# A vision transformer tower on one core: queries' and keys' product ahead of the payload's turn, and the exponential per tile

## The reference

```python
h = tokens(x)                                      # patches @ W.T + b, class token, + pos_embed
h = h + attention(layernorm(h))
h = h + experts(layernorm(h))

# attention, per head: window of 2 * 6 + 1 keys
scores = einsum('bnhd,bnwhd->bnhw', q, k_win) * D ** -0.5     # masked outside the image
out = einsum('bnhw,bnwhd->bnhd', softmax(scores), v_win).reshape(B, N, C) @ w_proj + b_proj

# experts
probs = softmax(flat @ router_w.T)
top_w, top_i = top_k(probs, 2)                     # normalised to sum 1
out = sum over e of w_e * (gelu(flat @ w1[e] + b1[e]) @ w2[e] + b2[e])
```

## Time and profile before

| | us |
|---|---|
| median of 3 runs | 1504.02 (1502.65 to 1506.02) |
| profiled execution | 1507.62 |
| its span | 1505.8 |
| busy in the span: TensorE | 1400.3 (93%) |
| VectorE | 1119.4 (74%) |
| GpSimd | 913.9 (61%) |
| ScalarE | 664.8 (44%) |

### The profile page before, as it was taken

How to read it: one execution, slowest core, us unless ns; L and a number is a source line. 1 busy time by engine, 2 the same in 40 slices (tenths; PEclk the granted TensorE clock), 3 DMA queues, 4 the chain that set the end, 5 groups by cost and what they waited for, 6 DMA issues and landing times.

```text
span 1505.8 us, 50706 instructions
## 1 busy us (share of the span) xinstructions
PE 1400.3 (93%) x17454; PEld 1165.2 (77%) x17455; DVE 1119.4 (74%) x2828; ACT 664.8 (44%) x1148; POOL 913.9 (61%) x902
## 2 busy tenths in 40 slices
PE   5899999999999999999788999999999999999995
PEld 5788788888888888888666677777777777777774
DVE  2578788898888888889677777666666666666663
ACT  2455555554555455455554434333333333333331
POOL 4235666666666667666367866666655666666565
PEclk9999999999999999999899999999999999999998
DMA  5565575767665675755355585555555555554553
GB/s 168 169 195 157 156 195 167 210 168 193 167 196 158 179 202 162 197 165 162 75 99 100 97 142 79 75 75 75 75 72 73 74 74 75 74 74 71 72 73 32
DMA packets 305660, 189.14 MB, mean 126 GB/s; under 512 B 201977, under 2 KB 291397, under 8 KB 304477
## 3 DMA queue, kind: packets, MB, share of 16 engines
q1 hardware_dynamic: 241706, 118.06, 32.2%
q0 software_dynamic: 41680, 41.84, 18.7%
q10 hardware_dynamic: 22115, 27.08, 5.7%
HBM read 89.79 MB, written 65.29 MB: 103 GB/s over the span
## 4 chain that ended last, share of the span: by engine, by line
PE 53%; DVE 23%; issue 8%; POOL 7%; DMA 3%; ACTq 2%; ACT 2%; SPq 1%; DVEq 0%; POOLq 0%
PE scores L1129 7%; PE qk L1146 7%; PE qk L1147 7%; PE qk L1148 7%; PE near L1129 5%; PE mixed L1129 3%; PE token_bank L1129 3%; PE far L1129 3%; PE qk L1251 3%; POOL sorted_scratch L527 3%; DVE st L778 3%; DVE qk L1030 2%; PE near L1182 2%; ACTq L628 2%; POOL payload L539 2%
## 5 line engine op out<-in xcount | busy, mean ns | idle before, releaser
L527 POOL DMA_INDIRECT sorted_scratch<-payload,place x212 | 222.9, 1051 | 56.6 <-issue 56.5
L1182 PE MATMUL near<-we,both_patches 128*120 128x192 f32 x1272 | 225.3, 335 | 18.4 <-DMA both_patches<-in_xt 11.7
L1182 PEld LDWEIGHTS near<-we,both_patches 128*120 128x120 f32 x1272 | 209.5, 186 | 29.1 <-issue 27.3
L512 POOL DMA_INDIRECT out<-both_patches,token x108 | 198.0, 1833 | 36.3 <-issue 36.2
L602 ACT ACTIVATE stage<-near,bias 128x384 f32<-128x384 f32 x103 | 60.0, 582 | 357.2 <-PE near L1129 332.8
L512 POOL DMA_INDIRECT out<-v_side,token x105 | 193.8, 1845 | 36.9 <-issue 36.5
L1146 PE MATMUL qk<-w_hi,stage 128*128 x666 | 164.2, 247 | 1.8 <-DVE v_side L940 1.7
L1146 PE MATMUL qk<-w_hi,both_patches 128*128 x648 | 160.0, 247 | 5.3 <-issue 4.6
L1148 PE MATMUL qk<-w_hi,we 128*128 x666 | 164.2, 246 | 0.0
L1147 PE MATMUL qk<-w_lo,stage 128*128 x666 | 164.2, 246 | 0.0
L1148 PE MATMUL qk<-w_hi,both_patches 128*128 x648 | 159.6, 246 | 0.0
(11 more groups left out here) (271 smaller groups left out, 3605.4 us busy)
## 6 DMA issues: line engine op xcount, KB each, us to landing
both_patches<-in_xt SPq DMA_DIRECT2D x53, 720.0 KB, 4.8
v_diag<-v_scratch SPq DMA_DIRECT2D x159, 89.2 KB
v_scratch<-v_side SPq DMA_DIRECT2D x53, 191.2 KB, 3.8
tabs<-tab_scratch SPq DMA_DIRECT2D x53, 180.0 KB, 4.8
out<-h ACTq DMA_DIRECT2D x52, 180.0 KB
stage<-in_w ACTq DMA_DIRECT2D x8, 1152.0 KB
k_diag<-qk SPq DMA_DIRECT2D x436, 15.8 KB
stage<-in_w ACTq DMA_DIRECT2D x8, 576.0 KB
```

What stands on the lines that cost most here:

```text
L512: pool.indirect_dma_start(out=out, out_offset=bass.IndirectOffsetOnAxis(ap=token[k][:, n:n + 1], axis=0), in_=y[k % 2][:, n, :], in_offset ...
L527: pool.indirect_dma_start(out=sorted_dram, out_offset=bass.IndirectOffsetOnAxis(ap=at, axis=0), in_=payload[0:rows, 2 * (block % RING) + n ...
L1182: ins = pe.matmul(near[0:ROWS, n * D:n * D + D], patches[f % 2][:, x, n * ROWS:n * ROWS + ROWS], we[:, x, :], start=(x == 0), stop=(x == K ...
```

## The change

In iterations t < 53 TensorE's order behind the turn of the probabilities becomes: queries' and keys' product, payload's turn, projection, router, values. The router writes into the `near` bank (the embedding's) instead of `far`: it waits until VectorE has read the embedding, the next embedding waits until the logits have been copied, and the projection no longer waits for the logits. ScalarE's order becomes: exponential, payload's cast, share, `features`, `attended`, queries' and keys' high half, `routed_features`, probabilities of tile 0, logits, probabilities of tile 1, values. In all iterations the exponential is two instructions, one per tile, each behind its tile's subtraction; TensorE turns each tile, and multiplies each tile's probabilities, behind its own semaphore count; and VectorE takes maximum and subtraction of tile 0 and then of tile 1, instead of two maxima and two subtractions. The transfers are the same. From t = 53 on the order of products is as before.

```diff
                 def exponentials():
-                    act.wait_ge(s["shifted"], 2 * (c + 1))
-                    act.activation(flat, flat, ACT.Exp, scale=DH ** -0.5 / (WS * WS)).then_inc(s["exp_set"], 1)
+                    for n in range(2):
+                        half = flat[:, n * HEADS * KEYS:(n + 1) * HEADS * KEYS]
+                        act.wait_ge(s["shifted"], 2 * c + n + 1)
+                        act.activation(half, half, ACT.Exp, scale=DH ** -0.5 / (WS * WS)).then_inc(s["exp_set"], 1)
...
+                def logits():
+                    if runs(t, 6):
+                        act.wait_ge(s["routed"], b + 1)
...
+                        act.mul(logit[:, at:at + 2, :], (near if t < BLOCKS else far)[0:ROWS, 0:2 * EXPERTS].rearrange("p (n e) -> p n e", n=2), 1.0 / WS)\
+                           .then_inc(s["logit_set"], 1)
+                def query_key_high():
+                    if runs(t, 1):
+                        act.wait_ge(s["qk_done"], g + 1)
+                        need(act, s["scored"], 2 * (g - 2))
+                        act.copy(qk16[g % QK_RING][:, :, 0, REACH:REACH + SPAN], qk[:, 0:3, 0:SPAN]).then_inc(s["qk_hi_set"], 1)
...
                     if runs(t, 5):
                         attended()
+                    query_key_high()
                     if runs(t, 6):
                         routed_features()
                     if runs(t, 4):
-                        probabilities()
+                        probabilities(0)
+                    logits()
+                    if runs(t, 4):
+                        probabilities(1)
...
                         dve.tensor_reduce(mx[:, n], scores[:, n, 0:HEADS * KEYS].rearrange("p (h c) -> p h c", c=KEYS), AX.X, ALU.max)\
                            .then_inc(s["max_set"], 1)
-                    need(dve, s["prob_turned"], 2 * a)
-                    for n in range(2):
+                        need(dve, s["prob_turned"], 2 * a - 1 + n)
                         dve.wait_ge(s["max_set"], 2 * a + n + 1)
                         dve.tensor_tensor(prob[:, n], ..., ALU.subtract).then_inc(s["shifted"], 1)
...
                     need(pe, s["h1_set"], f)
+                    need(pe, s["logit_set"], t - 6)
                     embed(0)
...
-                    pe.wait_ge(s["exp_set"], c + 1)
                     for n in range(2):
+                        pe.wait_ge(s["exp_set"], 2 * c + n + 1)
                         for m in range(QUADS):
                             ins = pe.transpose(scores[0:VKEYS, n, 128 * m:128 * m + 128], ...)
...
+                if t < BLOCKS:
+                    queries_keys()
+                    turn_routed()
+                    project()
+                    route()
+                    make_values()
+                else:
+                    turn_routed()
+                    queries_keys()
+                    early(3)
+                    route()
+                    make_values()
+                    early(4)
+                    project()
+                    early(5)
...
-                    pe.wait_ge(s["p_set"], 2 * (c + 1))
                     pe.wait_ge(s["v_in"], VDMA * (c + 1))
...
                     for n in range(2):
+                        pe.wait_ge(s["p_set"], 2 * c + n + 1)
```

More of the change, by code:

```diff
@@ L702, in body @@
                     if runs(t, 4):
-                        probabilities()
+                        probabilities(0, 1)
                     if runs(t, 6):
@@ L706, in body @@
                     early(3)
[L707 to L714, removed]
+                if t >= BLOCKS:
+                    logits()
+                    query_key_high()
                 if runs(t, 1):
-                    act.wait_ge(s["qk_done"], g + 1)
-                    need(act, s["scored"], 2 * (g - 2))
-                    act.copy(qk16[g % QK_RING][:, :, 0, REACH:REACH + SPAN], qk[:, 0:3, 0:SPAN]).then_inc(s["qk_hi_set"], 1)
                     act.wait_ge(s["v_done"], g + 1)
@@ L1233, in body, with turn_routed @@
                     ins.then_inc(s["counted"], 1)
-                if runs(t, 6):
-                    pe.wait_ge(s["lo2"], b + 1)
+                def turn_routed():
+                    if runs(t, 6):
+                        pe.wait_ge(s["lo2"], b + 1)
+                        if runs(t, 1):
+                            pe.wait_ge(s["xT_set"], g + 1)
+                        else:
+                            pe.wait_ge(s["v_set"], BLOCKS)
+                            pe.wait_ge(s["xT2_set"], b)
+                        slot_of = 2 * (b % RING)
+                        turn(payload[:, slot_of:slot_of + 2, :].bitcast(F16), token_bank[:].bitcast(F16), lambda n, c: (3 * n + c) * ROWS)\
+                            .then_inc(s["turned2"], 1)
@@ L1237, in body, with queries_keys @@
+                def queries_keys():
                     if runs(t, 1):
                         pe.wait_ge(s["xT_set"], g + 1)
[L1239 to L1253, removed]
@@ L1254, in body @@
-                early(3)
-                if runs(t, 6):
-                    pe.wait_ge(s["xT2_set"], b + 1)
+                        need(pe, s["qk_main"], g)
+                        for j in range(3):
+                            for i, (x, w, half) in enumerate(PRODUCTS):
+                                ins = pe.matmul(qk[:, j, 0:SPAN], wqk[half][:, w, 128 * j:128 * j + 128], xT1[:, x, :],
+                                                start=(i == 0), stop=(i == len(PRODUCTS) - 1))
+                        ins.then_inc(s["qk_done"], 1)
@@ new lines, in route @@
+                def route():
+                    if runs(t, 6):
+                        pe.wait_ge(s["xT2_set"], b + 1)
+                        if t < BLOCKS:
+                            pe.wait_ge(s["h1_set"], t + 1)
+                        elif runs(t, 5):
+                            pe.wait_ge(s["oT_set"], d + 1)
+                        else:
+                            pe.wait_ge(s["h2_set"], BLOCKS)
+                        for n in range(2):
+                            for j, (x, w, half) in enumerate(PRODUCTS):
+                                ins = pe.matmul((near if t < BLOCKS else far)[0:ROWS, n * EXPERTS:(n + 1) * EXPERTS], xT2[:, n, x, :], wr[half][:, w, :],
+                                                start=(j == 0), stop=(j == len(PRODUCTS) - 1))
+                        ins.then_inc(s["routed"], 1)
@@ new lines, in make_values, with project @@
+                def make_values():
+                    if runs(t, 1):
+                        for n in range(2):
+                            for j, (x, w, half) in enumerate(PRODUCTS):
+                                ins = pe.matmul(token_bank[0:ROWS, n * D:n * D + D], xT1[:, x, n * ROWS:n * ROWS + ROWS], wv[half][:, w, :],
+                                                start=(j == 0), stop=(j == len(PRODUCTS) - 1))
+                        ins.then_inc(s["v_done"], 1)
+                def project():
@@ L1258, in body @@
                     if runs(t, 5):
                         pe.wait_ge(s["oT_set"], d + 1)
[L1260 to L1285, removed]
@@ L1286, in body @@
-                early(5)
+                        if t >= BLOCKS:
+                            pe.wait_ge(s["logit_set"], b + 1)
+                        for n in range(2):
+                            dst = far[0:ROWS, n * D:n * D + D]
+                            pe.matmul(dst, ones16[:, 0:ROWS], bp[:], start=True, stop=False)
+                            for j, (x, w, half) in enumerate(PRODUCTS):
+                                ins = pe.matmul(dst, oT[:, x, n * ROWS:n * ROWS + ROWS], wp[half][:, w, :], start=False, stop=(j == len(PRODUCTS) - 1))
@@ new lines, in project @@
+                        ins.then_inc(s["proj_done"], 1)
+                if t < BLOCKS:
+                    queries_keys()
[3 more added lines that the diff above has]
+                    make_values()
+                else:
+                    turn_routed()
[6 more added lines that the diff above has]
+                    early(5)
```

8 lines of the change are left out of this document (6 added, 2 removed).

## The result

The changed kernel takes 1536.12 us in the median (1529.52 to 1537.91, 4 runs) against 1505.02 us (1502.65 to 1509.55, 4 runs): a ratio of 1.0192, 95% interval 1.0164 to 1.022, some 29 us slower by the ratio (31 by the medians). Its profiled execution took 1534.99 us, with a span of 1533.2 us.

What follows compares the result with a forecast made beforehand. The prediction took a two-iteration loop from exponential through router logits and VectorE's selection to bound the kernel; 26.2 + 5.1 - 8 - 2 = +21 us on 1504.02 gave about 1525 us, with an 8-in-10 range of 1506 to 1542.

Steps and rivals of the forecast that it cites:

- the step that the prediction put first: Two attention iterations form one loop, 28.33 us; its 5.26 us from exponential to VectorE's selection count in full once per pair.
- The selection's start: VectorE's selection in odd iterations starts about 6.40 us behind the exponential instead of 5.26: +1.14, 23 times, +26.2 us.
- The replaced waits: On TensorE, the product waits for the features instead of the payload; the router waits 0.25 us for the second features' copy.
- VectorE's order: Alternating maximum and subtraction on VectorE costs two waits of 0.11 us per loop, 23 times: +5.1 us, bounds 0 and 8.
- The edge copies: VectorE's 24-column copies stall behind GpSimd; half of the 23 even iterations lose the stall: -8 us, bounds -25 and 0.
- The condition that the prediction named: In even iterations the copy's stall stays where the exponential follows VectorE's result by 0.3 us or more sooner than 3.24.
- the wait for the counts: VectorE's wait for the counts, 2.5 us in four places, goes because TensorE's transposes are earlier: -2 us.
- VectorE's wait for the logits: Sign in the profile after: this wait grows from 11.3 us to over 30; if not, TensorE was the bound.
- TensorE's pace: Rival: TensorE sets the pace, so its earlier first tile and vanished payload wait win 17 us, 1487 us; chance 0.12.
- The stalls that go everywhere: Rival: line 1036's copy slips ahead of GpSimd in odd iterations too, giving back 25.4 us: +4, 1508 us; chance 0.1.
- The much slower case: Rival: no copy stall goes and TensorE is late starting the product: +40 us, 1544 us; chance 0.1.

## Why the prediction was right, point by point

Faster or slower was decided by the step that the prediction put first, and it held: the loop runs through the logits. The sum was 21 us and the measured change 29 (25 to 33), inside the range.

**The selection's start.** Predicted 2.26 for the product, 5.47 for the router and 6.40 for the selection; the rows show 2.25, 5.47 and 6.44. Over all 23 odd iterations the mean from exponential to selection went from 5.47 to 6.64 us (from the starts of the two in the trace), 1.16 each, 26.8 in sum; predicted 26.2. The replaced waits are the ones that were named.

**VectorE's order.** The term was mis-sized: the two waits took 8.6 us instead of 5.1. The prediction took an instruction that waits to start 0.04 us behind its predecessor's end; the subtraction starts 0.11 behind it (422.95 + 0.67, then 423.73), 0.78 behind the maximum's start instead of 0.59, so 0.19 at each of two places and not 0.11. The sum of the times from each maximum's start to the next instruction rose by 8.6 us in VectorE's part of the 22 loops. The Trainium skill, "VectorE: DVE Perf Modes", section "The DRAIN you can't avoid", has its figure from eight copies, and it doesn't carry over to this pair of a reduction and a subtraction that waits for it.

But 4.8 us of it came back at once, by a stall that the prediction had at nothing. The router's normalisation follows the odd iteration's subtractions on VectorE (count, busy, mean ns; first before, then after):

```profile
L790 DVE TENSOR_SCALAR xn<-h,mv,rs 120x192 f32<-120x192 f32 x88 | 38.1, 472 | 0.0
```

```profile
L807 DVE TENSOR_SCALAR xn<-h,mv,rs 120x192 f32<-120x192 f32 x88 | 29.2, 374 | 0.0
```

Before, in 21 of the 22 loops, the first of its two instructions there took 0.59 us and ended 0.06 behind GpSimd's indexed store (line 527). In the changed kernel it comes 0.39 us later, when that store is nearly over, and takes 0.37. The traces show the same 4.8 us, one way or the other, between the kernel before and the one with the split alone, and in the two pairs with the new order of products that differ in the order on VectorE (the changed kernel against two maxima first, and against the split undone). The waits' net price was thus some 4 us.

**The edge copies.** Predicted -8, by an estimate that half of the even iterations would lose the stall. Of the trace: odd iterations kept it (0.66 us on average before, 0.63 after), even ones went from 0.81 to 0.44, together -8.9 us in the 22 loops. The condition that the prediction named held in all 23 even iterations of the changed kernel: the copy stalled in the 9 whose exponential followed VectorE's result by 2.93 us or less, and not in the 14 where that was 2.97 or more. The group of the copy after (count, busy, mean ns):

```profile
L1053 DVE COPY qk<-qk 128x24 f16<-128x24 f16 x44 | 23.1, 524 | 0.0
```

**What was missing.** That the sum came near is in part luck, since terms that it had at nothing cancel. From the first of the 23 selections to the last the changed kernel took 634.5 us against 612.3, so its 22 loops are 22.2 us longer: 25.4 by the selection's later start (of the 26.8, without the first), 3.4 between VectorE's result and the exponential, and -6.5 in VectorE's part. In that part stand 8.6, -8.9 and -2 from the sum's terms; what the sum lacked are the normalisation's -4.8, -2.3 in the choice of the second expert (line 827 in even iterations; where it is long, it ends 0.06 us behind GpSimd's instruction of the payload's low half), and +3 spread over small ones. The rest of the 27.4 us between the two profiled spans lies outside these loops: 1.8 ahead of them and 3.4 behind.

Two terms made the time longer and stood for nothing in the sum. The four key DMAs and what else lies between VectorE's result and the exponential took 3.18 us on average instead of 3.03, which is 3.4 us over 22 loops. I have no cause for it; in the kernels with one half of the change it was 3.00 and 3.09. And behind the attention iterations the profiled execution took 4 us longer, in stretches in which the same work was done at a lower granted clock. The experts' second batch and its fifth, first after, then before (stretch, busy times, then the granted clock as a share):

```profile
781.00:802.20 21.20, 18.33 (x246) 13.68 (x246) 15.94 (x46) 10.66 (x18) 9.55 (x10) 0.92 0.42 98
...
837.50:857.30 19.80, 16.26 (x118) 12.61 (x119) 8.47 (x20) 5.63 (x11) 12.77 (x10) 0.74 0.36 57
```

```profile
756.30:776.30 20.00, 16.73 (x246) 12.79 (x246) 15.71 (x47) 10.47 (x17) 9.63 (x11) 1.00 0.51 99
...
811.40:828.50 17.10, 13.48 (x118) 10.56 (x119) 8.52 (x20) 5.62 (x11) 12.77 (x10) 0.90 0.38 65
```

The instructions are as many (118 and 118 matmuls) and TensorE waits the same 3.4 us for the payload in the last of them, but the granted clock, a mean between its two levels (1.2 and 2.4 GHz, the latter being 1.00), was 0.74 instead of 0.90, and the stretch took 2.7 us longer. In the first of them the waits grew too, by 0.9 us for the payload and 0.5 for a transfer. Whether the change has a part in the clock is open. Of its four runs, three had a mean granted clock of 0.980 to 0.982 and took 1535 to 1538 us, and the one at 0.985 took 1529.5; the variants with two copies exchanged, with the maxima first and with the edge copies rewritten ran at 0.983 to 0.988. So a few of the microseconds that these win over the changed kernel may be the clock's; their loops in the traces, 11.9, 12.2 and 17.8 us shorter, say that most are not.

The smaller terms went as said: the wait for the counts fell from 2.5 to 0.9 us. VectorE's wait for the logits, which was to grow to over 30 us, grew to 29.5.

**The rivals.** TensorE's pace is out (the split alone was slower, and TensorE's gain became a wait for the payload). The stalls that go everywhere did not go in odd iterations. The much slower case, in which TensorE itself is late, appears in single iterations (in 10 of the 23 the product starts 2.46 to 2.87 us behind the exponential instead of 2.25, and the selection at 6.6 to 7.05) and is in the mean.

## What to carry to other kernels

Follow the loop that closes across iterations before counting any engine's waits: a wait that is filled with work moved ahead is only won if what now comes later isn't what another engine, working in order, stands still for. When such a loop is found, look first at the waiting engine's own order: putting ready work ahead of the wait won 2.4% here (about a third of it by an edge copy that then no longer met GpSimd's instruction), and it did harm where the work put ahead was not ready. And where a short instruction takes several times its own duration, see which engine's instruction ends with it: moving such an instruction by a few tenths of a microsecond can bring the stall or take it away, as the normalisation shows, so an order's price is read from the whole loop and not from one wait.

## What the runs showed of the hardware

A copy of 24 columns on VectorE, 0.16 us by itself, lasts, where it meets one of GpSimd's instructions, until that one ends (737 ns on average before); written as a maximum over one element it takes 168 ns in the same place. The Trainium skill, "SBUF — State Buffer", section "Who interferes with whom", says that copies in VectorE's two-port modes are shut out while a GpSimd instruction holds the port pair that the two engines share, that instructions with two inputs from SBUF contend with a GpSimd instruction that reads SBUF, and that one with a single input outside those modes does not. The rows agree with all three: the copy stalls, the selection's step with two inputs stalls (0.72 us instead of 0.19), and the reduction does not. In which mode the copies run, no run shows. The stalls were worth 23 us of 1507, for instructions whose own work is 0.16 us.
